# First and scan stage: xd rests, gate tiles, the order of the u, du and C loads, and the B product in half banks

## The reference, cut to what matters

```python
x_ = einsum('ed,bld->bel', in_proj_w, context)            # 1024 channels, 1024 steps, 4 batches
u = silu(causal_conv4(x_) + conv_b)
x_dbl = einsum('ke,bel->bkl', x_proj_w, u)                # 32 low-rank rows, 16 of B, 16 of C
delta = softplus(einsum('er,brl->bel', dt_proj_w, x_dbl[:, :32]) + dt_proj_b)
A = -exp(A_log)                                           # channel x 16 states
# for every channel e, state n and step t:
state = state * exp(delta[t] * A) + (delta[t] * u[t]) * B[t]
y[t] = sum over n of state * C[t]
y = (y + D * u) * silu(z)                                 # z is the layer norm of x
x = x + tanh(g_xattn) * y
```

## Time and profile before

| | us |
|---|---|
| runs | 4153.29, 4159.72, 4159.78 |
| median | 4159.72 |
| profiled execution | 4151.87, span 4149.8 |
| first stage | 0 to 492 |
| scan stage | 492 to 1746 |
| third stage | 1746 to 4150 |
| PE busy in the span | 3843.5 (93%) |
| DVE busy | 3046.5 (73%) |
| ACT busy | 2147.3 (52%) |
| POOL busy | 1721.3 (41%) |

### The profile page before, as it was taken

The page is one execution under the profiler, slowest core; times in us unless marked ns, Lnnn a source line. Parts: engine busy times, 40 slices in busy tenths (PEclk is TensorE's granted clock), DMA queues, the critical chain, the costliest instruction groups (busy, mean ns, idle before and its releaser), DMA issues. The chain is left out here.

```text
span 4149.8 us, 59457 instructions
## 1 busy us (share of the span) xinstructions
PE 3843.5 (93%) x21088; PEld 3146.5 (76%) x21088; DVE 3046.5 (73%) x3711; ACT 2147.3 (52%) x2256; POOL 1721.3 (41%) x977
## 2 busy tenths in 40 slices
PE   8898588898898898799999989999999999999999
PEld 3444478788788788678888868888888888788887
DVE  7888789999999999877777745555555555455555
ACT  3777689898899898722222234444444444200000
POOL 0233189999999999823333310000000000122222
PEclk9999599999999999899999989999999999999999
DMA  6677843643643643455555646767766666677543
GB/s 234 243 283 251 294 142 105 182 147 104 187 138 109 182 137 118 138 185 177 185 182 184 223 167 235 242 235 241 242 233 235 229 235 232 226 278 264 196 164 117
DMA packets 328294, 819.57 MB, mean 197 GB/s; under 512 B 65920, under 2 KB 109696, under 8 KB 318784
## 3 DMA queue, kind: packets, MB, share of 16 engines
q1 hardware_dynamic: 296240, 750.13, 52.9%
q0 software_dynamic: 31744, 67.23, 5.5%
q10 hardware_dynamic: 144, 0.00, 0.0%
HBM read 603.38 MB, written 245.27 MB: 205 GB/s over the span
## 5 line engine op out<-in xcount | busy, mean ns | idle before, releaser
L1095 POOL TENSOR_TENSOR h<-h,c 128x1024 f32<-128x1024 f32 x512 | 1205.3, 2410 | 38.1 <-DVE h L1078 34.6
L1078 DVE TENSOR_TENSOR_SCAN h<-da,dbu 128x1024 f32<-128x1024 f32 x512 | 1134.8, 2273 | 68.2 <-ACT dbu L1041 39.3
L1048 ACT ACTIVATE da<-dl,ad 128x1024 f32<-128x1024 f32 x512 | 588.4, 1149 | 82.5 <-DVE h L1078 69.3
L1126 PE MATMUL psy<-ident,h 128*128 128x128 f32 x4096 | 562.5, 281 | 44.2 <-POOL h L1095 24.7
L1041 ACT ACTIVATE dbu<-psb 128x1024 f32<-128x1024 f32 x510 | 520.8, 1021 | 72.2 <-PE psb L1116 64.1
L2032 DVE TENSOR_TENSOR wsp<-arena,wsp 128x2048 fp32r<-128x2048 f32 x198 | 447.7, 2289 | 100.4 <-ACT wsp L1984 100.4
L1126 PEld LDWEIGHTS psy<-ident,h 128*128 128x128 f32 x4096 | 447.9, 143 | 77.7 <-POOL h L1095 50.0
L1870 POOL DMA_INDIRECT xg<-scratch_xn,ids x64 | 63.3, 990 | 1032.0 <-PE psT L1888 1010.7
L1984 ACT ACTIVATE wsp<-arena 128x2048 fp32r<-128x2048 f32 x198 | 370.2, 1909 | 23.8 <-DMA arena<-in_w 23.4
L1116 PE MATMUL psb<-m,du_taps 128*128 128x128 f32 x2048 | 288.7, 288 | 63.6 <-ACT dbu L1041 63.4
L1116 PEld LDWEIGHTS psb<-m,du_taps 128*128 128x128 f32 x2048 | 251.5, 193 | 101.1 <-ACT dbu L1041 96.1
(11 more groups left out here) (215 smaller groups left out, 7911.9 us busy)
## 6 DMA issues: line engine op xcount, KB each, us to landing
arena<-in_w SPq DMA_DIRECT2D x192, 1024.0 KB, 6.9
du_taps<-scratch_duT SPq DMA_DIRECT2D x496, 128.0 KB, 2.9
c<-scratch_c SPq DMA_DIRECT2D x64, 512.0 KB, 8.2
scratch_xT<-xT_s SPq DMA_DIRECT2D x32, 1024.0 KB, 4.9
scratch_ob<-ob SPq DMA_DIRECT2D x64, 512.0 KB, 2.6
xT_place<-scratch_xT SPq DMA_DIRECT2D x32, 1024.0 KB, 6.3
scratch_duT<-duT SPq DMA_DIRECT2D x52, 512.0 KB, 4.0
xz<-in_x SPq DMA_DIRECT2D x32, 512.0 KB, 5.6
```

What stands on the lines that cost most here:

```text
L1048: act.activation(da[k % 2][:, :], dl[:, i % 2, :], ACT.Exp, scale=ad[:, i % 2, n:n + 1]).then_inc(s_da, 1)
L1078: dve.tensor_tensor_scan(h[:, k % HR, :], da[k % 2][:, :], dbu[:, (k // GN) % 2, k % GN, :], 0.0, ALU.mult, ALU.add).then_inc(s_scan, 1)
L1095: pool.tensor_tensor(h[:, k % HR, :], h[:, k % HR, :], c[:, n, :], ALU.mult).then_inc(s_hc, 1)
L1126: mm = pe.matmul(psy[:, t, :], h[:, k % HR, t * P:(t + 1) * P], ident[:], is_transpose=True, start=(n == 0 and t % 4 == 0), stop=(n == NST ...
```

## The change

In the first stage DVE does the rests of xd ahead of du_rest in a batch turn's step, and gate tile 29 is gated in step 30 instead of 29 (tile 28 stays in step 29). In the scan stage SP loads five C tiles, u of the first unit, the second matrix half and then eleven C tiles; in the last unit of a batch it loads the first matrix half, two C tiles, du, the gate and then six C tiles. The B product is done in halves: four matmuls into one bank, a semaphore step, four into the other, a step; ACT copies each half as soon as it is there, and a half of the next product waits only for the copy of the same half. s_mm and s_ev count twice as far, so all waits on them are doubled.

```diff
--- before.py
+++ after.py
@@ -146,8 +146,10 @@
                 a = 1 + 3 * (g // 2) + g % 2
                 return (a, a), (a + 1, a + 1)
             a = 13 + (g - ET) * 5 // 2
+            if a + 3 >= Q:
+                return (a, a), (a + 1, a + 1)
             if a + 3 >= Q - 1:
-                return (a, a), (a + 1, a + 1)
+                return (a, a), (a + 1, a + 2)
             return (a, a + 1), (a + 2, a + 3)
 
         counted = {ZG * g + i: (z_steps(g)[0][i], z_steps(g)[1][i]) for g in range(Q // ZG) for i in range(ZG)}
@@ -793,6 +795,9 @@
                                   ALU.subtract).then_inc(s_btlo, 1)
 
             def step(s):
+                b = batch_at(s, 1)
+                if b is not None:
+                    xd_rest(b)
                 on_tile(s, DUT, du_rest)
                 if s == Q - 1:
                     convolve(s)
@@ -804,9 +809,6 @@
                     for k in (1, 3):
                         dve.tensor_tensor(w_dts[k * DR:(k + 1) * DR], w_dt[k * DR:(k + 1) * DR],
                                           f32(w_dts[k * DR:(k + 1) * DR]), ALU.subtract).then_inc(s_wdlo, 1)
-                b = batch_at(s, 1)
-                if b is not None:
-                    xd_rest(b)
                 b = batch_at(s, 3)
                 if b is not None:
                     b_rest(b)
@@ -870,10 +872,12 @@
         SETS = NU * NST
         PARTS = 4
         CP = NC // PARTS
+        CH = CP // 2
         HR = 4
         AHEAD, BEHIND = 3, 6
         GATED, SKIPPED = 1, 6
         GATED_AT = 8
+        FIRST = 5
         skip = sb("skip", [P, P])
         gate = sb("gate2", [P, 1])
         m0, m1 = m0[:], sb("m", [P, TB * ROW], F32R)[:]
@@ -933,7 +937,7 @@
 
             def load_du(i, r):
 
-                after(sp, s_mm, (i - 1) * NST + NST - PARTS + r + 1 if i else 0)
+                after(sp, s_mm, 2 * ((i - 1) * NST + NST - PARTS + r + 1) if i else 0)
                 for part in range(2):
                     for twin in range(2):
                         sp.dma_start(f32(duT[part * 2 * TB + twin:(part + 1) * 2 * TB:2, r * CP:(r + 1) * CP, :]),
@@ -942,7 +946,7 @@
             def load_m(b, half):
 
                 if b:
-                    sp.wait_ge(s_mm, (b * ET - 1) * NST + (half + 1) * NH)
+                    sp.wait_ge(s_mm, 2 * ((b * ET - 1) * NST + (half + 1) * NH))
                 else:
                     sp.wait_ge(s_zero, 1)
                 for dst_, src_ in matrix_blocks(f32((m0, m1)[half]).rearrange("p (t r) -> p t r", t=TB), dr, b, half):
@@ -969,7 +973,7 @@
 
             def first_weights():
 
-                sp.wait_ge(s_mm, (NU - 1) * NST + NH)
+                sp.wait_ge(s_mm, 2 * ((NU - 1) * NST + NH))
                 for mat, src_ in enumerate((io["w_sg"], io["w_su"])):
                     for half in range(2):
                         w0 = (2 * mat + half) * KH * HB // 2
@@ -978,7 +982,7 @@
 
             def first_tokens():
 
-                sp.wait_ge(s_mm, SETS)
+                sp.wait_ge(s_mm, 2 * SETS)
                 sp.wait_ge(s_gst, 16 * ET)
                 for t in range(2):
                     for i, src_ in enumerate((dr["gated"], io["x"])):
@@ -986,10 +990,11 @@
                         sp.dma_start(arena[:, w0:w0 + H], src_.rearrange("b (t p) h -> (b t) p h", p=P)[t]).then_inc(early["x"][t], 16)
 
             load_delta(0)
-            for n in range(3):
+            for n in range(FIRST):
                 load_c(0, n)
+            load_u(0)
             load_m(0, 1)
-            for n in range(3, NST):
+            for n in range(FIRST, NST):
                 load_c(0, n)
 
             for i in range(NU):
@@ -1006,15 +1011,14 @@
                         load_c(b, n)
                 if i:
                     store(i - 1)
-                load_u(i)
+                    load_u(i)
                 if turned:
                     for n in range(12, NST):
                         load_c(b, n)
                 if turn:
-                    for n in range(6):
+                    load_m(b, 0)
+                    for n in range(2):
                         load_c(b, n)
-                if turn:
-                    load_m(b, 0)
                 for r in range(PARTS):
                     if not final:
                         load_du(i + 1, r)
@@ -1023,7 +1027,7 @@
                     first_weights()
                     first_tokens()
                 if turn:
-                    for n in range(6, 8):
+                    for n in range(2, 8):
                         load_c(b, n)
             store(NU - 1)
 
@@ -1036,10 +1040,13 @@
                 if k >= SETS:
                     return
                 g, r = k // GN, k % GN
-                act.wait_ge(s_mm, k + 1)
                 after(act, s_scan, (g - 1) * GN)
-                act.activation(dbu[:, g % 2].rearrange("p n (t c) -> p n t c", c=NC)[:, :, :, r * CP:(r + 1) * CP],
-                               product_bank(k).rearrange("p c t n -> p n t c"), ACT.Copy).then_inc(s_ev, 1)
+                for half in range(2):
+                    act.wait_ge(s_mm, 2 * k + half + 1)
+                    c0 = r * CP + half * CH
+                    act.activation(dbu[:, g % 2].rearrange("p n (t c) -> p n t c", c=NC)[:, :, :, c0:c0 + CH],
+                                   product_bank(k)[:, half * CH:(half + 1) * CH].rearrange("p c t n -> p n t c"),
+                                   ACT.Copy).then_inc(s_ev, 1)
 
             def unit(i, n, k):
                 if n == 0:
@@ -1072,7 +1079,7 @@
 
             def unit(i, n, k):
                 dve.wait_ge(s_da, k + 1)
-                dve.wait_ge(s_ev, (k // GN) * GN + GN)
+                dve.wait_ge(s_ev, 2 * ((k // GN) * GN + GN))
 
                 after(dve, s_ys, k - HR + 1)
                 dve.tensor_tensor_scan(h[:, k % HR, :], da[k % 2][:, :], dbu[:, (k // GN) % 2, k % GN, :], 0.0, ALU.mult,
@@ -1111,10 +1118,11 @@
                     pe.wait_ge(early["m"], 2 * TB // BAND * 16)
                 elif k % (ET * NST) in (0, NH):
                     pe.wait_ge(s_m[half], (i // ET + half) * 2 * TB // BAND * 16)
-                after(pe, s_ev, k - 1 if k <= GN else k)
-                for j in range(CP):
-                    mm = pe.matmul(product_bank(k)[:, j], duT[:, r * CP + j, :], m[g // 2][:, :, r * CP + j, g % 2 * GN:(g % 2 + 1) * GN], start=True, stop=True)
-                mm.then_inc(s_mm, 1)
+                for half in range(2):
+                    after(pe, s_ev, 2 * ((k - 1 if k <= GN else k) - 1) + half + 1)
+                    for j in range(half * CH, (half + 1) * CH):
+                        mm = pe.matmul(product_bank(k)[:, j], duT[:, r * CP + j, :], m[g // 2][:, :, r * CP + j, g % 2 * GN:(g % 2 + 1) * GN], start=True, stop=True)
+                    mm.then_inc(s_mm, 1)
 
             def add_state(k):
 
```

## The result

Six runs of the changed kernel had a median of 4132.37 us (4129.42 to 4135.99), six of the kernel before beside them 4152.48 (4144.08 to 4159.78): a ratio of 0.9949, interval 0.9938 to 0.9960, some 20 us less. The forecast was 4127, with a gain of 31. The profiled execution took 4133.35 (span 4131.3), 18.5 us less than the one of before.

What follows compares the result with a forecast made beforehand. POOL's product was taken to bound the scan, busy 1212 of 1254 us. Gains 7.7 + 14.7 + 3.0 + 1.2 + 4.1 = 30.7 us gave 4121.2 from the profiled run, 4129.0 from the median; forecast 4127, range 4110 to 4150.

Steps and rivals of the forecast that it cites:

- The u load, 7.7: Scan start: u tile loaded earlier, so PE's 8.18 us wait for aux and POOL's 7.70 us idle spell go.
- the filling, 1.2: First unit: half products and copies start the first scan 0.4 us sooner and save 0.8 before the fifth product.
- The batch turns, 14.7: Three batch turns in the scan: du loads go out sooner, removing POOL's idle spells, 5.66 us at the first, 9.0 at the others.
- the small spells, 3.0: Scan stage: half of POOL's remaining 6.3 us of small idle spells goes, those right behind a long one; ends 0 and 6.3.
- Rival C: Turns only half cured: du's last part, C row 2 or the starting matrix late; 8 to 10 us less gain, 4138; chance 0.12.
- The halves, apart from the filling, 0: Scan's steady state: half products and copies cost or gain 0, hidden beside POOL; up to 31 us more ACT time.
- The first stage, 4.1: Before the scan: xd rests ahead of du_rest gain 1.0 and 1.7 us, gate tile 29 moved to step 30 gains 1.4.
- aux gone: Sign of being right: PE no longer waits for aux, the u tile, in unit 0.
- du under 1 us: Sign of being right: PE waits for du_taps at the batch turns are none or under 1 us.
- copies of about 0.60 us: Sign of being right: ACT's 1024 dbu copies in the scan take about 0.60 us each.
- POOL idle 8 to 10 us: Sign of being right: POOL's idle time in the scan falls to 8 to 10 us, from 34.6.
- scan 1227 us: Sign of being right: the scan stage is near 1227 us long, from 1254.

## Why the prediction was right, and where it was not

Direction and range held, and the mechanisms named for the first unit and the first stage are there. The gain was 18.5 us in the profiled executions, where I had summed 30.7. That the total fell into the range is in part luck: 17.7 us of the sum were the turns, which gave next to nothing, and what makes up for some of it, the halves behind late transfers and a larger gain in the first stage, was not in the sum.

**The u load, 7.7, and the filling, 1.2: the mechanism right, the exact sum luck.** No wait for aux is left in unit 0, and in this pair of profiles unit 0 is 8.9 us shorter, the sum of the two, of which 1.2 go with the halves by the run without them. But with the same code unit 0 took 40.10 to 43.52 us, and 48.47 to 49.68 before, so the gain is 4.9 to 9.6. I had set the matrix at the start at 0, upper end 3; PE waits for it 0.68 us in the changed kernel and up to 2.88 in others with the same start.

**The batch turns, 14.7, and the small spells, 3.0: the step that failed.** It reads: "What waits behind du now: silu [...] and C rows 2 to 7", with 5 us of slack for row 2. The rows were in time (POOL waits for none). What I left out is that the second half of the matrix stands behind these rows too; I had looked at the matrix only at the start of the stage. It is issued at 795.44 behind six rows, wanted by PE at 806.5, and came at 812.1. Measured: 2.1 us over the six units, which is less than they move by with the same code, and 1.0 over the rest of the stage (12.5 - 8.9 - 2.1 = 1.5, of which 0.5 before the first product). Its deeper fault is one of method. I asked for each moved transfer whether it was late, never what the turn has to carry in all. The DMA engines are busy 0.84 of the 78 us around the turn against 0.36 in a steady unit, and 0.86 to 1.09 in every 5 us from 790 to 815. With a full queue an order chooses who is late; the runs with three other orders and with the rows on ACT's queue, and the changed kernel with fewer bytes, show it. Rival C had the kind of cause ("du's last part or C row 2 comes late [...] or the matrix at the start"), and a gain of 22, nearer the measured 18.5 to 20; I had given it 0.12.

**The halves, apart from the filling, 0: too low.** In the kernel before I would have been right (a ratio of 0.9996), in the changed one they are worth 8.4 us of scan stage by one pair of profiles, 8 by the ratios and 4.4 by the medians. I priced them for a steady unit and one filling, not for every refill behind a late transfer. This hid part of the failed step: without them the changed kernel's scan stage is 4.0 us shorter than that of before, though unit 0 alone gained 7.7, and the turns are longer (245.8 us against 242.9). ACT's own time rose by 9.9 us over the stage, less than the 31 I had allowed, beside POOL as said. The Trainium skill's 26 ns for every increment (the section that the prediction weighs; it gives the figure for small tiles packed into the array, each with an increment of its own, which these products are not) would be 13 us on the path; the kernel before with halves, with 512 more increments, was not slower in its scan stage (1247.0 against 1250.4), which agrees with their lying beside POOL. No run measured an increment.

**The first stage, 4.1: mis-sized, 7.2 measured by the pair of profiles.** By the measure of the table it is 9.7: the eight kernels with this code stand at -5.4 to -11.0 at tile 31, -9.0 in the mean, three with the code of before at +0.7. The rests were mis-sized: 1.6 and 3.6 us at their two steps instead of 1.0 and 1.7, of which 1.1 are PE's clock, which I had left out of the sum, though 0.69 and 0.63 stood in the trace of the kernel before; and they gain more behind, up to 2.1 us from tile 17 to 24 and 2.4 at the end. The gate tile brought 2.5 instead of 1.4 alone, and nothing that can be told from the drift beside the rests.

**The signs I had named**: aux gone, yes; du under 1 us, no (7.7, but none longer than 2.2); copies of about 0.60 us, yes (590 ns); POOL idle 8 to 10 us, no (23.0); scan 1227 us, no (1241.6 by the same measure); first stage 3 to 5 us shorter, more.
